# Attention scores by one VectorE instruction each, a mean by TensorE, a last tile's layer norm on VectorE

## The reference

```
# layer 0
scores = where(adj > 0, x @ weight @ input.T, -2**32)
x  = layernorm(x + softmax(scores / 0.07, axis=1) @ input)
# layer 1, on the x just made (x1 below)
Wh = x @ W;  s1 = Wh @ a1;  s2 = Wh @ a2
e  = leaky_relu(s1[:, None] + s2[None, :], 0.2)
h  = elu(softmax(where(adj > 0, e, -9e15), axis=1) @ Wh)
x  = layernorm(x + h)
```

## Time and profile before

| | |
|---|---|
| median of 3 runs | 1458.09 us (1456.67 to 1458.68) |
| the profiled execution: its time, its span | 1458.37 us, 1456.6 us |
| busy over the span: PE, DVE, POOL, ACT | 97%, 86%, 84%, 73% |
| mean granted clock of PE | 0.989 |

### The profile page before, as it was taken

One profiled execution on the slowest core, in us unless ns is written; L12 is line 12 of the kernel. 1 busy time (PEld: TensorE's weight loads), 2 busy tenths in 40 slices (PEclk: granted clock), 3 DMA queues, 4 the chain that ended last, 5 costly groups with the idle time before them and its releaser, 6 DMA issues.

```text
span 1456.6 us, 28346 instructions
## 1 busy us (share of the span) xinstructions
PE 1411.4 (97%) x9661; PEld 1010.5 (69%) x9661; DVE 1253.8 (86%) x2129; ACT 1066.9 (73%) x2435; POOL 1217.3 (84%) x906
## 2 busy tenths in 40 slices
PE   8799999999999999999999999979999999999995
PEld 4577777777777777777777777755666666666664
DVE  6799999999999899999999999849898897979794
ACT  6688888888888888888888888868755555545453
POOL 6978888888888888888888888838999999999995
PEclk9999999999999999999999999988999999999998
DMA  8799999999999999999999998673434343434420
GB/s 267 243 286 261 271 253 266 273 266 275 273 256 264 249 272 267 270 271 271 266 256 265 261 261 268 185 140 66 107 68 103 85 102 85 104 67 111 76 58 14
DMA packets 427918, 291.38 MB, mean 200 GB/s; under 512 B 356864, under 2 KB 403200, under 8 KB 427776
## 3 DMA queue, kind: packets, MB, share of 16 engines
q1 hardware_dynamic: 427776, 289.59, 73.0%
HBM read 160.56 MB, written 40.89 MB: 138 GB/s over the span
## 4 chain that ended last, share of the span: by engine, by line
PE 92%; DVE 2%; POOL 2%; issue 1%; ACT 1%; DMA 1%; SPq 0%; POOLq 0%; ACTq 0%; DVEq 0%
PE ps L594 16%; PE ps L680 13%; PE ps L673 12%; PE ps L620 11%; PE ps L596 8%; PE ps L633 8%; PE ps L632 8%; PE ps L631 8%; PE ps L657 6%; PE ps L691 1%; POOL edges L426 1%; PE ps L564 1%; DVE rows L934 1%; POOL inp_sb L416 1%; POOL vals L419 0%
## 5 line engine op out<-in xcount | busy, mean ns | idle before, releaser
L798 ACT ACTIVATE rows<-rows,exp_bias 128x512 f32<-128x512 f32 x576 | 417.2, 724 | 58.2 <-DVE exp_bias L987 58.2
L505 POOL TENSOR_TENSOR p_lo<-p,p_hi 128x1024 fp32r<-128x1024 f32 x180 | 423.7, 2395 | 21.8 <-ACT p_hi L832 11.5
L934 DVE CUSTOM_DVE_ANT_0 rows<-ps,neg_mask 128x1024 f32<-128x1024 f32 x288 | 352.2, 1223 | 81.9 <-PE ps L633 71.1
L1014 DVE SCALAR_TENSOR_TENSOR p<-ps,e_col,edgesT 128x1024 f32<-128x1024 f32 x288 | 349.6, 1276 | 53.4 <-PE ps L650 36.5
L426 POOL TENSOR_SCALAR edges<-neg_mask 128x1536 uint8<-128x1536 bf16 x192 | 311.2, 1621 | 92.7 <-DVE neg_mask L909 80.7
L832 ACT CAST p_hi<-p 128x1024 fp32r<-128x1024 f32 x180 | 185.1, 1047 | 166.5 <-DVE p L1014 163.9
L594 PE MATMUL ps<-vals,pT_hi 128*128 128x256 f16 x1536 | 295.9, 273 | 3.1 <-DVE pT_lo L943 2.1
L784 ACT CAST pT_hi<-ps 128x512 f16<-128x512 f32 x384 | 222.7, 580 | 93.2 <-PE ps L620 93.0
L457 POOL TENSOR_TENSOR inp_sb<-rows,inp_sb 128x512 f16<-128x512 f32 x192 | 279.5, 1475 | 10.5 <-ACT inp_sb L792 2.9
L596 PE MATMUL ps<-vals,pT_lo 128*128 128x128 f16 x1536 | 275.1, 219 | 0.0
L943 DVE TENSOR_TENSOR pT_lo<-ps,pT_hi 128x512 f16<-128x512 f32 x384 | 250.8, 683 | 11.7 <-ACT pT_hi L784 11.7
(11 more groups left out here) (110 smaller groups left out, 1853.1 us busy)
## 6 DMA issues: line engine op xcount, KB each, us to landing
adj_sb<-adj SPq DMA_DIRECT2D x192, 768.0 KB, 5.7
edge_rows<-edges SPq DMA_DIRECT2D x192, 192.0 KB, 4.8
xq<-x SPq DMA_DIRECT2D x48, 64.0 KB, 2.9
xr<-x SPq DMA_DIRECT2D x48, 64.0 KB, 5.8
out<-y_w SPq DMA_DIRECT2D x5, 512.0 KB, 3.6
inp_sb<-inp SPq DMA_DIRECT2D x3, 768.0 KB, 8.2
inp_sb<-inp_sb SPq DMA_TRANSPOSE x96, 4.7
edgesT<-edge_rows SPq DMA_TRANSPOSE x48, 5.3
```

The source lines that it names most:

```text
L505: nc.gpsimd.tensor_tensor(p1_lo[:, m % LO_SLOTS, :], p1[:, (NB * g + n) % P_SLOTS, :], p1_hi[:, m % HI_SLOTS, :].bitcast(F32), ALU.subtrac ...
L798: nc.scalar.activation(row_chunk(1 - par, c), row_chunk(1 - par, c), ACT.Exp, bias=exp_bias[:, 1 - par:2 - par], scale=EXP_SCALE, accum_ou ...
L934: nc.vector.tensor_tensor_reduce(row_pair(par, k), scores_pair(k), neg_mask_row[:, 2 * k * CHUNK:2 * (k + 1) * CHUNK], 1.0, -3.0e38, ALU.a ...
L1014: nc.vector.scalar_tensor_tensor(out=p1[:, (NB * g + n) % P_SLOTS, :], in0=ps[:, R_ROW:R_ROW + 2, :].rearrange("p b w -> p (b w)"), scalar ...
```

## The change

1. `score_cols` on POOL and `score_sums` on ACT go. On DVE, at c = 1 (`SUMS_STEP`) of loop steps t = 3 to 49, `score_sums(t - 3)` makes each of the two products together with its sum in one instruction (`tensor_tensor_reduce`); the last tile's pair comes behind the loop.
2. The running sum `x1_total` goes. PE adds up the column sums of x1 in PSUM (`mean_part`): 46 products of a 128x128 block of x1 with one column in loop step t = 48, four ahead of each chunk's other work, and the last two in `mean_of_wh`. The sum lies in bank 7, from which DVE reads it spread over 128 columns; bank 6 takes bank 7's place among the banks of the weighted values.
3. For the last tile (t = 49) the two additions and the normalization move from POOL to DVE; the power stays on POOL.

```diff
-        VALS_BANKS = (2, 3, OUT3)
+        VALS_BANKS = (2, 3, SPARE)
+        mean_ps = ps[:, OUT3, 3 * P:3 * P + 1]
...
-            def score_cols(j):
-                pool.wait_ge(x1_set, j + 1)
-                x1 = x1_all[:, j, :]
-                pool.wait_ge(wa_copied, 1)
-                after(pool, s_set, j)
-                nc.gpsimd.tensor_tensor(s_prod[:], x1.rearrange("p (a d) -> p a d", a=1).to_broadcast([P, 2, P]), wa_rep[:],
-                                        ALU.mult).then_inc(s_prod_set, 1)
-                if j == 0:
-                    nc.gpsimd.tensor_copy(x1_total[:], x1).then_inc(total_set, 1)
-                else:
-                    pool.wait_ge(total_set, j)
-                    nc.gpsimd.tensor_tensor(x1_total[:], x1_total[:], x1, ALU.add).then_inc(total_set, 1)
...
-                if ends_tile(known):
+                if t == NB + 1:
+                    pool.wait_ge(ve_set, NB)
+                    nc.gpsimd.tensor_tensor(small[:, 4:5], small[:, 3:4], consts[:, 0:1], ALU.pow).then_inc(rstd_set, 1)
+                elif ends_tile(known):
...
-                    score_cols(tile)
...
+            def mean_part(j):
+                pe.wait_ge(x1_set, j + 1)
+                return nc.tensor.matmul(mean_ps, x1_all[:, j, :], averager[:, 0:1], start=(j == 0), stop=(j == NB - 1),
+                                        skip_group_check=True)
+
             def tile_steps(t, par, known):
                 for c in range(C):
+                    if t == NB:
+                        for j in range(4 * c, min(4 * c + 4, NB - 2)):
+                            mean_part(j)
...
             def mean_of_wh():
-                pe.wait_ge(total_set, NB)
-                nc.tensor.matmul(ps[:, SPARE, 0:P], x1_total[:], averager[:], start=True, stop=True).then_inc(mean_turned, 1)
+                mean_part(NB - 2)
+                mean_part(NB - 1).then_inc(mean_turned, 1)
                 pe.wait_ge(mean_repd, 1)
-                nc.tensor.matmul(ps[:, SPARE, P:2 * P], mean_rep[:], w1_c[:, 0:P], start=True, stop=True).then_inc(mean_made, 1)
+                nc.tensor.matmul(ps[:, OUT3, P:2 * P], mean_rep[:], w1_c[:, 0:P], start=True, stop=True).then_inc(mean_made, 1)
...
-            def score_sums(j):
-                act.wait_ge(s_prod_set, j + 1)
-                for k in range(2):
-                    op = nc.scalar.activation(s_prod[:, k, :], s_prod[:, k, :], ACT.Copy, accum_out=s_cols[:, k, j:j + 1])
-                op.then_inc(s_set, 1)
...
-                    if c == 4 and t >= 3:
-                        score_sums(t - 3)
-                    if c == C - 1 and t == NB + 1:
-                        score_sums(t - 2)
...
+            def score_sums(j):
+                dve.wait_ge(x1_set, j + 1)
+                dve.wait_ge(wa_copied, 1)
+                after(dve, s_set, 2 * j)
+                for k in range(2):
+                    nc.vector.tensor_tensor_reduce(s_prod[:, k, :], x1_all[:, j, :], wa_rep[:, k, :], 1.0, 0.0, ALU.mult,
+                                                   ALU.add, s_cols[:, k, j:j + 1]).then_inc(s_set, 1)
...
+                    if c == SUMS_STEP and t >= 3:
+                        score_sums(t - 3)
...
+                        if c == ATT_STEP + 1 and t == NB + 1:
+                            dve.wait_ge(att_out, NB)
+                            dve.wait_ge(xr_in[par], 16 * (t // 2))
+                            nc.vector.tensor_tensor(xr[:, par, :], att[:, 0:P], xr[:, par, :], ALU.add).then_inc(u1_set, 1)
+                            dve.wait_ge(u1_set, NB)
+                            nc.vector.tensor_tensor(xr[:, par, :], att[:, P:2 * P], xr[:, par, :], ALU.add).then_inc(u_set, 1)
...
-            dve.wait_ge(s_set, NB)
+            dve.wait_ge(rstd_set, NB)
+            nc.vector.tensor_scalar(x1_all[:, NB - 1, :], xr[:, (NB - 1) % 2, :], moments[:, 0:1], small[:, 4:5], ALU.subtract,
+                                    ALU.mult).then_inc(x1_set, 1)
+            score_sums(NB - 1)
+            dve.wait_ge(s_set, 2 * NB)
...
-                nc.vector.tensor_scalar(mean_rep[:], ps[:, SPARE, 0:P], 1.0 / NB, None, ALU.mult).then_inc(mean_repd, 1)
+                nc.vector.tensor_scalar(mean_rep[:], mean_ps.to_broadcast([P, P]), 1.0 / NB, None, ALU.mult).then_inc(mean_repd, 1)
```

More of the change, by code:

```diff
@@ L74, in build @@
         x1_all = sb("x1_all", [P, NB, P], F32)
-        x1_total = sb("x1_total", [P, P], F32)
         s_prod = sb("s_prod", [P, 2, P], F32)
@@ L237, in build @@
         edgesT_in = [sem(f"edgesT_in{i}") for i in range(PART_SLOTS)]
-        s_prod_set, s_set, total_set = sem("s_prod_set"), sem("s_set"), sem("total_set")
+        s_set = sem("s_set")
         s_part, s_spread, s_all = sem("s_part"), sem("s_spread"), sem("s_all")
@@ L269, in build @@
         ATT_STEP = LAG + PV_LAG + MOVED
+        SUMS_STEP = 1
         def turn_of(t, c):
@@ L1027, in mean_steps @@
                 dve.wait_ge(mean_turned, 1)
-                nc.vector.tensor_scalar(mean_rep[:], ps[:, SPARE, 0:P], 1.0 / NB, None, ALU.mult).then_inc(mean_repd, 1)
+                nc.vector.tensor_scalar(mean_rep[:], mean_ps.to_broadcast([P, P]), 1.0 / NB, None, ALU.mult).then_inc(mean_repd, 1)
                 dve.wait_ge(mean_made, 1)
-                nc.vector.tensor_copy(mean_wh[:], ps[:, SPARE, P:2 * P]).then_inc(mean_set, 1)
+                nc.vector.tensor_copy(mean_wh[:], ps[:, OUT3, P:2 * P]).then_inc(mean_set, 1)
                 dve.wait_ge(mean_set, 1)
```

## The result

| | before | after |
|---|---|---|
| median us (lowest to highest of 6 runs each) | 1458.35 (1456.6 to 1459.2) | 1464.85 (1464.09 to 1465.22) |
| span of the profiled execution, us | 1456.6 | 1463.1 |
| granted clock of PE, mean | 0.989 | 0.992 |

The ratio of after to before is 1.0046, 95% interval 1.0035 to 1.0058: slower by 0.46%, some 6.5 us. The forecast was 1464.9, which was 6.8 us on top of the 1458.09 known then.

The account below looks back on a forecast made before the run. PE was taken to bound the kernel, with 92% of the span. On the profiled 1458.37 us, +4.5 + 4.0 - 1.9 + 0.2 gave 1465.2, less 0.3 for the median 1464.9 us; range 1459.5 to 1478.5.

Parts of the forecast that it names:

- DVE's price and slack: First-stage loop: two sums cost DVE 0.42 us a tile against 0.32 slack, so PE stalls 0.10 us a tile, +4.5 us.
- Step 48: Loop step t = 48, no scores left: 46 mean products at 0.24 us make PE the bound, +4.0 us.
- The end of the stage: Chain after the first stage's last attention output: the last tile's work on DVE shortens it, -1.9 us.
- Stage two: Two last mean products stand where PE is the bound, in place of one of 128 columns, +0.2 us.
- Rival 1: Loop tiles: DVE's slack holds and PE never waits, only +2.3 us remain, 1460.4 us; chance 20%.
- Rival 2: Step 48: mean products vanish into PE's holes, decided below 0.154 us a product, no DVE stall, 1454.0 us; chance 10%.
- Rival 3: DVE's sum instruction runs at half rate, 0.35 us each, a stall of 0.38 us in 45 tiles, 1477.8 us; chance 15%.
- Rival 4: PE's clock falls in step 48 under one-column products, +1.7 to +11 us on the forecast, 1466 to 1476 us; chance 8%.

Follow-up runs that it names:

- e2_sums_apart: Changed kernel with one of the two sum instructions left at chunk 1 and the other moved to chunk 10: 1460.77 us, ratio 1.0019 to the kernel before.
- e3_sums_twice: Changed kernel with both sum instructions run twice at chunk 1, the extra pair into tiles nothing reads: 1484.33 us, ratio 1.0182 to the kernel before.
- e6_sums_by_pool_act: Changed kernel with the score products back on POOL and their sums back on ACT: 1461.38 us, ratio 1.0025 to the kernel before.
- e9_spread_in_holes: Against e8_apart_spread: step 48's mean products four a chunk at c = 3 to 9, 16 behind the last attention products, four behind the first spread of r: 1458.04 us.
- e5_mean_by_pool: Changed kernel with the running sum x1_total back on POOL and one mean product on PE: 1461.35 us, ratio 1.0026 to the kernel before.
- e7_last_tile_on_pool: Changed kernel with only the last tile's additions and normalization back on POOL: 1466.43 us (two runs), ratio 1.0059 to the kernel before.
- e8_apart_spread: Against e2_sums_apart: mean products spread, 24 in step 48, 14 behind the last attention products, 8 behind the first spread of r, 2 in stage two: 1456.21 us.
- e10_products_twice: Changed kernel with each one-column mean product of step 48 run twice, the second into an unread PSUM column: 1501.0 us, ratio 1.0288 to the kernel before.
- e1_sums_at_c10: Changed kernel with both sum instructions moved from chunk 1 to chunk 10 of each tile: 1480.29 us, ratio 1.0152 to the kernel before.
- e4_sums_at_c5: Changed kernel with both sum instructions moved from chunk 1 to chunk 5 of each tile: 1563.99 us, ratio 1.0729 to the kernel before.

## Why the prediction was right, step by step

- **DVE's price and slack: right.** d = 0.42 was forecast and 2 x 0.21 measured; the transposes of c = 9 wait 0.09 us for `pT_lo` (0.10 forecast). e2_sums_apart and e3_sums_twice show both sides of the bend: d = 0.21 costs nothing in a tile, d = 0.85 costs 0.43 more than d = 0.42. The stall is worth 4.1 us (e2_sums_apart), forecast 4.5. e6_sums_by_pool_act, with no sums on DVE, has a tile of 19.35 us again.
- **Step 48: right mechanism, size off.** PE is the bound there as forecast (21.62 of 21.62 us), but a product takes 0.215 us (0.86 for four, the 1.52 between two groups in e9_spread_in_holes less 0.66), not 0.24, and the term was +3.2, not +4.0; e5_mean_by_pool gives 3.5 with the two products in stage two. The row I sized it by, 0.12 us a pass, has 129 columns a pass; with one column a pass takes 0.84 / 8 = 0.105. With 46 of them the sum of the prediction gives 21.3; the other 0.3 are the eight groups with transposes, which take 2.00 us each instead of 0.86 + 0.44 + 0.66 = 1.96. The lower bound in the text, 0.22 a product from the transposes' loads, was the row to take. The Trainium skill's rule in the prediction (TensorE: Matmul & The Clock Gate, section LDWEIGHTS), by which a product would be 0.21 us, is what the trace shows.
- **The end of the stage: right,** -1.9 forecast and measured, of which 0.88 is the move of the last tile's work (e7_last_tile_on_pool).
- **Stage two:** +0.2 forecast, +0.5 measured. The products in `mean_of_wh` are 0.35 us (1009.10) in place of one of 128 columns (0.24), for +0.1. The rest is the clock, which the prediction did not count here. In before it stands at 0.51 from 978.5 to 992.2 us, in after at 0.50 from 988.7 to 998.9. So the transpose of `s_top` escapes it in after (0.31 us instead of 0.46), and 6.13 us pass from `s_top` to the first products instead of 6.29; but 5.1 us of the products lie at half clock instead of some 4.1. In the chain of before the second group of products (L680, from 990.00) takes 2.77 us, in that of after (L678, from 995.88) 3.31.
- **The sum was right in part by luck.** The four terms came to +4.8, +3.2, -1.9 and +0.5 between the two traces, instead of +4.5, +4.0, -1.9 and +0.2: errors that cancel. Of the 4.8 some 0.5 had arisen before any sum ran (the first layer-norm statistics at 80.52 us instead of 80.06), and this start varies by more among the other kernels (79.72 to 81.37). The forecast was +6.8 on a median that later came out 0.3 higher, and +6.5 was measured; that 1464.9 and 1464.85 agree to 0.05 us is luck.
- **Rival 1, slack holds:** refuted, though close: it holds at 0.21 us a tile and not at 0.42.
- **Rival 2, hidden products:** refuted for 46 of them at 0.215 us, but the mechanism is real. With 24 in the step and most others in PE's idle time at the end (e8_apart_spread) their cost is gone: 1456.21 us, where the kernel before less the 1.9 us of the last chain would be at 1456.2. The rival's other half, the clock of a busier PE, came true (1.00 in step 48 instead of 0.91), but with PE as the bound of a longer step it saved nothing against the forecast.
- **Rival 3, half rate:** refuted. Both sources are f32 in SBUF, and the instructions start 0.21 us apart, what rows 3 and 6 gave for the full rate. The rule that the prediction named there (Trainium skill, Vector Engine (DVE) Microarchitecture Reference, section 7) does not hold for this instruction. The page states it for one instruction shape, `S2S2D2_STT`; the trace lists the sums as CUSTOM_DVE_ANT_0, and no run here shows whether that is the shape.
- **Rival 4, the clock:** it did not fall in step 48 (1.00 over 21.62 us). It is not far: twice the products bring it down (e10_products_twice).
- **Not foreseen:** the prediction counted POOL's work against a mask (1.56 us instead of 0.95), but not against the sums. At c = 1 POOL happens to be idle, so nothing came of it; at c = 10 and c = 5, where one theory each had free slack, it cost 15 and 99 us more than at c = 1.

## What to carry to other kernels

Work taken off engines that bound nothing gives nothing back in the loop, and work put on an engine with 9% idle time costs as soon as the local slack ahead of the next consumer is used up. Measure that slack in one tile's timeline (here 0.32 us) and keep what stands in it below; the split of e2_sums_apart made both sums free in the loop. Look at what POOL does at the place where a two-input DVE instruction is put, and at where the instructions behind it move. Here a product of one column cost nearly as much as one of 129 (0.105 against 0.12 us a pass); put such products where PE is idle by itself, and count how many fit. And compare two traces at a point ahead of the change first: here they differed by up to 1.65 us at 80 us, more than several of the effects sought.

## What the runs showed of the hardware

- A DVE product-with-sum of 128x128 from two f32 SBUF sources takes 0.21 us from start to start, and its record grows from 0.28 to 1.21 and 1.54 us when a POOL instruction that reads SBUF began shortly ahead of it. A mask of 128x1536 takes 0.95 us alone and up to 2.23 beside POOL; in five cases of before, after, e1_sums_at_c10 and e4_sums_at_c5 it ended 0.81 or 0.82 us behind the POOL instruction under way at its start.
- An f32 product of one column is two passes of 0.105 us at a granted clock of 1.00, and 0.40 us in all at half clock.
- A PE that is busy without a gap can lose its clock: after 11.90 us with twice the one-column products among transposes and attention products the granted clock went to 0.51 for 41.4 us (e10_products_twice), while with half as many such products it stayed at 1.00 over 21.62 us. In the kernel before, with none and PE busy for 14.63 of 18.50 us, it was 0.91.
